# Four orders in the QKV stage: when rows are loaded and normalised, where two transposes stand, and when keys are split

## The reference

```python
x = x + _L0_xattn_ref(_layernorm(x, axis=-1), ...)
...
def rat_read(res, W, gamma, beta, num_outputs):
    x = res.reshape(b, l, H, C)                      # H = 512, C = 4
    y = jnp.einsum('blhc,hoc->bloh', x, W)
    mu = y.mean(-1, keepdims=True)
    var = y.var(-1, keepdims=True)
    yn = (y - mu) * jax.lax.rsqrt(var + EPS)
    yn = yn * gamma.reshape(num_outputs, H) + beta.reshape(num_outputs, H)
...
qkv_in = rat_read(hidden_states, attn_read_w, attn_read_g, attn_read_b, 3)
q, k, v = jnp.split(qkv_in, 3, axis=-1)
q = jnp.einsum('bli,oi->blo', q, qkv_w[0]).reshape(b, l, NH, HD)   # and k, v alike; NH = 16, HD = 32
q = rope(q, pos)
k = rope(k, pos)
```

## Time and profile before

| | us |
|---|---|
| median of 3 runs | 2207.84 |
| lowest and highest run | 2196.89, 2216.57 |
| the profiled execution | 2209.95 |
| its span, first to last instruction | 2208.0 |
| PE busy | 2082.5 (94%) |
| DVE busy | 1489.1 (67%) |
| ACT busy | 1085.5 (49%) |
| POOL busy | 1165.4 (53%) |

### The profile page before, as it was taken

How to read it: one execution, slowest core, us unless ns; L and a number is a source line. 1 busy time by engine, 2 the same in 40 slices (tenths; PEclk the granted TensorE clock), 3 DMA queues, 4 the chain that set the end, 5 groups by cost and what they waited for, 6 DMA issues and landing times.

```text
span 2208.0 us, 32471 instructions
## 1 busy us (share of the span) xinstructions
PE 2082.5 (94%) x11176; PEld 1702.9 (77%) x11176; DVE 1489.1 (67%) x1982; ACT 1085.5 (49%) x1700; POOL 1165.4 (53%) x717
## 2 busy tenths in 40 slices
PE   6988889999997999799999999999889999999999
PEld 4777766666665888688888899999678878888877
DVE  6787766777775999445655526776876675757663
ACT  3444447888895888621322336666633232323221
POOL 0111127899897888400000068776666676666564
PEclk9999997999998999899999999999999999999999
DMA  5678763333323766377998648778988699897895
GB/s 191 210 236 254 234 211 97 103 102 103 106 75 114 284 246 236 144 252 247 312 324 267 231 175 303 295 286 308 335 327 294 227 314 333 279 308 251 269 310 198
DMA packets 259994, 518.21 MB, mean 235 GB/s; under 512 B 21081, under 2 KB 136793, under 8 KB 241282
## 3 DMA queue, kind: packets, MB, share of 16 engines
q1 hardware_dynamic: 259842, 516.24, 69.9%
HBM read 360.45 MB, written 155.45 MB: 234 GB/s over the span
## 4 chain that ended last, share of the span: by engine, by line
PE 74%; DVE 8%; DMA 5%; ACT 5%; issue 4%; POOL 3%; SPq 1%; DVEq 0%; POOLq 0%; ACTq 0%
PE s_m_psG L2359 8%; PE s_m_psU L2359 8%; PE s_psF L2955 7%; PE s_psF L2957 7%; PE s_psF L2956 7%; PE s_psO L923 6%; PE s_w_psA L1923 4%; PE s_w_psB L1923 4%; PE s_psS L868 4%; PE s_psX L898 3%; DMA s_f_xs<-xnT 2%; PE s_psQ L575 2%; PE s_psQ L577 2%; PE s_psQ L576 2%; PE s_psY L559 2%
## 5 line engine op out<-in xcount | busy, mean ns | idle before, releaser
L1068 POOL TENSOR_TENSOR s_a_pl<-s_a_pf,s_a_ph 128x1024 fp32r<-128x1024 f32 (+1 forms) x128 | 279.8, 2214 | 35.0 <-ACT s_a_pf L1024 34.9
L2911 POOL TENSOR_TENSOR s_f_xs<-s_f_xl,s_f_xs 128x1024 f32<-128x1024 f32 x80 | 204.1, 2551 | 147.5 <-DMA s_f_xs<-xnT 147.2
L2095 POOL TENSOR_TENSOR s_w_yl<-s_w_y,s_w_yh 128x1024 fp32r<-128x1024 f32 x32 | 76.1, 2404 | 366.1 <-ACT s_w_yh L2003 366.1
L951 DVE TENSOR_REDUCE s_a_mx<-s_psS 128x1 f32<-128x896 f32 (+2 forms) x248 | 179.3, 754 | 77.7 <-PE s_psS L874 77.6
L2784 ACT ACTIVATE s_f_xh<-s_f_xs 128x1024 fp32r<-128x1024 f32 x80 | 84.9, 1061 | 291.0 <-POOL s_f_xs L2911 289.1
L2835 DVE TENSOR_TENSOR s_f_xl<-s_f_xs,s_f_xh 128x1024 fp32r<-128x1024 f32 x80 | 110.0, 1375 | 163.4 <-ACT s_f_xh L2784 163.4
L2955 PE MATMUL s_psF<-s_f_wh,s_f_xh 128*128 128x512 f32 x448 | 175.7, 392 | 8.1 <-DVE s_f_acc L2852 7.5
L448 POOL TENSOR_TENSOR s_q_qk<-s_q_ra,s_q_rb 128x1024 f32<-128x1024 f32 x16 | 37.8, 2361 | 275.2 <-DVE s_q_rb L691 275.2
L2957 PE MATMUL s_psF<-s_f_wh,s_f_xl 128*128 128x512 f32 x448 | 174.9, 390 | 0.0
L2956 PE MATMUL s_psF<-s_f_wl,s_f_xh 128*128 128x512 f32 x448 | 174.9, 390 | 0.0
L1021 ACT ACTIVATE s_a_ph<-s_psX 128x1024 fp32r<-128x1024 f32 (+1 forms) x160 | 150.2, 939 | 43.8 <-PE s_psX L903 40.0
(11 more groups left out here) (332 smaller groups left out, 6340.0 us busy)
## 6 DMA issues: line engine op xcount, KB each, us to landing
s_f_xl<-xnT SPq DMA_DIRECT2D x112, 512.0 KB, 5.3
s_f_xs<-xnT SPq DMA_DIRECT2D x80, 512.0 KB, 6.9
s_q_xt<-xT SPq DMA_DIRECT2D x16, 1024.0 KB, 7.4
s_q_xc<-xP SPq DMA_DIRECT2D x16, 1024.0 KB, 10.0
hsD<-s_q_hs SPq DMA_DIRECT2D x16, 1024.0 KB, 4.8
s_w_hin<-hsD SPq DMA_DIRECT2D x16, 1024.0 KB, 4.9
hs<-s_w_res SPq DMA_DIRECT2D x16, 1024.0 KB, 4.7
s_m_raw<-giT SPq DMA_DIRECT2D x32, 512.0 KB, 5.4
```

The source lines that it names most:

```text
L951: dve.tensor_reduce(mx[:, slot % 2, qi:qi + 1], psS[:, off:off + (qi + 1) * P], AX, ALU.max).then_inc(mx_ok, 1)
L1068: pool.tensor_tensor(pl[:, r, cols], pf[:, j - 1, 0:n], ph[:, r, cols], ALU.subtract).then_inc(pl_ok, 1)
L2911: pool.tensor_tensor(xs[i % 3][:], xl[u % 4][:].bitcast(F32), xs[i % 3][:], ALU.add if product(u)[1][1][2] > 0 else ALU.subtract).then_inc ...
```

## The change

Four orders of work change; no instruction is added or removed. SP loads xc of a tile as the first thing of a step, as soon as `hs_ok` of tile s-2 frees the buffer, and no longer behind the store of hs and the load of xt; each load now has a semaphore of its own. ACT runs `first_norm` in front of the split of the third output, and both parts of q and k are split in front of the outputs' square root. PE has the first two transposes between read 0 and read 1. DVE splits q and k in front of the rotation.

```diff
@@ sync
             def body(s, p, live):
+                if live(0):
+                    if (s - 2).exists():
+                        sp.wait_ge(hs_ok, count(s - 2, 1, 1))
+                    sp.sem_inc(k["settled"], 1)
+                    sp.dma_start(xc[:, p], io["xP"][ds(s.at(P), P), :]).then_inc(xc_in[p], 16)
                 if live(2):
                     sp.wait_ge(hs_ok, count(s - 2, 1, 1))
...
                         sp.wait_ge(y_mm, count(s - 2, 4, 4))
                     sp.sem_inc(k["settled"], 1)
-                    tok = s.at(P)
-                    sp.dma_start(xt[:, p], io["xT"][:, :, ds(tok, P)]).then_inc(x_in[p], 16)
-                    sp.dma_start(xc[:, p], io["xP"][ds(tok, P), :]).then_inc(x_in[p], 16)
+                    sp.dma_start(xt[:, p], io["xT"][:, :, ds(s.at(P), P)]).then_inc(xt_in[p], 16)
+                if live(0):
                     if at_slot(s, 0):
                         sp.dma_start(wraw[:], io["wqkv"]).then_inc(w_in, 16)
@@ scalar
                     hi_y(s, 1)
+                if live(1):
+                    first_norm(s, 1 - p)
                 if live(2):
                     hi_y(s, 2)
-                if live(1):
-                    first_norm(s, 1 - p)
                 if live(3):
                     hi_qk(s, 0)
+                    hi_qk(s, 1)
                 if live(1):
                     act.wait_ge(y_norm, count(s - 1, 11, Y_SQ))
...
-                if live(3):
-                    hi_qk(s, 1)
                 if live(2):
                     act.wait_ge(qkv_mm, count(s - 2, 3, 3))
@@ tensor
-                    pe.wait_ge(x_in[1 - p], dma_count(s - 1, 2, 2))
+                    pe.wait_ge(xt_in[1 - p], dma_count(s - 1, 2, 1))
...
                 if live(1):
                     read(s, p, 0)
-                    read(s, p, 1)
                 if live(2):
                     turn_y(s, 0)
                     turn_y(s, 1)
+                if live(1):
+                    read(s, p, 1)
+                if live(2):
                     project(s, 0)
@@ vector
-                dve.wait_ge(x_in[p], dma_count(s, 2, 2))
+                dve.wait_ge(xc_in[p], dma_count(s, 2, 1))
...
                        .then_inc(sh_ok, 1)
+                if live(3):
+                    lo_qk(s, 0)
+                    lo_qk(s, 1)
                 if live(2):
...
-                if live(3):
-                    lo_qk(s, 0)
-                    lo_qk(s, 1)
```

More of the change, by code:

```diff
@@ L389, in build_qkv @@
         Y_LESS, Y_AGG, Y_VAR, Y_INV, Y_SQ = 2, 8, 9, 10, 11
-        x_in = [sem(f"x_in{p}") for p in range(2)]
+        xt_in = [sem(f"xt_in{p}") for p in range(2)]
+        xc_in = [sem(f"xc_in{p}") for p in range(2)]
         y_mm = sem("y_mm")
```

## The result

| | before | with the change |
|---|---|---|
| median, us | 2210.06 (4 runs) | 2179.95 (4 runs) |
| lowest and highest run | 2196.89, 2216.57 | 2172.20, 2183.38 |
| the profiled execution | 2209.95 | 2178.96 |
| its span | 2208.0 | 2177.2 |
| steps 3 to 16, 14 of them | 242.06 | 210.43 |

The ratio of the medians is 0.9864, with a 95% interval of 0.9823 to 0.9904: 1.4% faster. The span became 30.8 us shorter.

A forecast was written before the change was run, and what follows sets the result against it. No engine filled the QKV steps (PE 88% busy); PE and DVE waited, largely for late xc. Terms -29.3 - 1.8 - 1.4 + 1.7 = -30.8 from 2209.95 gave 2179.1 us; it named 2178, range 2166 to 2200.

The forecast's parts named there:

- case A: Whole kernel: the forecast itself comes true, own range 2168 to 2188 us, chance 0.56.
- The step: QKV steps 3 to 16: 17.29 us falls to 15.03 at full clock, 15.2 taken; 14 steps give -29.3 us.
- Late normalisation as the cause of late xc: QKV step: xc's load waits for ACT's normalisation, done at T+12.9; moved, it runs T+3.0 to T+5.1, 7.8 us sooner.
- DVE's slack: QKV step: DVE's chain ends at T+17.05, its next split stands at T+17.18, slack 0.13 us, the tightest place.
- Rival B: QKV steps: DVE's chain becomes the bound, the keys' split wait returns every second step, step 15.97, 2190 us; chance 0.19.
- The rule on DMA order: SP's DMA queue: descriptors of a ring go in order, so hsD behind xc lands 4.8 to 10.0 us after issue.
- C: QKV steps: DMA engines become the bound, DVE waits again, steps about 16.5, 2197 us; chance 0.07.
- E: QKV steps: the hs buffer's loop closes late behind a 12.97 us xc issue, step 20.4, 2254 us; chance 0.04.
- Start: First steps: the second xc goes ahead of xt, the chain behind starts sooner, -1.4 us, bounds 0 and -2.0.
- Step 17: Outside the stretch, with step 2: each gets the reads' or psB gain, 0.88 us, together -1.8, bounds 0 and -3.
- Handoff: End of QKV: last rotations stand behind the key split, PE's wait for POOL grows 1.51 to 3.2, +1.7 us.
- rival D: Handoff to attention: longer wait lengthens PE's half-clock stretch by 20 us, +10 us allowed, 2188 us; chance 0.10.

The follow-up runs named there:

- the rows edit: Kernel before, plus only xc loaded first and the normalisation ahead of the third output's split: 2192.77 us, ratio 0.9925.
- the runs without reads: Changed kernel with read 1 back ahead of the two transposes, 2193.29 us; kernel before with only xc's load and the normalisation moved, 2192.77 us.
- the normalisation late: Changed kernel with only ACT's normalisation back behind the third output's split, xc still loaded first: 2183.95 us, ratio 0.9876.
- DVE's chain longer: Changed kernel plus two unused 128x256 DVE additions between the keys' split and the rotations, in steps that also load a tile: 2184.03 us.
- rows and normalisation undone: Changed kernel with xc loaded last again and the normalisation behind the third output's split: 2205.36 us, ratio 0.9976.
- reads undone: Changed kernel with read 1 back ahead of the two transposes: 2193.29 us, ratio 0.9925.
- the store of hs last: Changed kernel with the store of hs moved behind the load of xt: 2179.3 us (1 run).
- the change again: The changed kernel unaltered, run again beside the handoff kernels: 2178.40 us, ratio 0.9854.
- the products that kept PE at work: Changed kernel plus 24 unused products of the identity with itself on PE ahead of the last key transposes: 2178.09 us, ratio 0.9868.

## Why the prediction was right

It named 2178 us, with 2166 to 2200 around it, and 2179.95 was measured; by the medians the gain is 30.1 us, where 2207.84 - 2178 = 29.8 was forecast. The likeliest case A is what happened, for the reasons given. By its steps:

**The step.** Forecast T+2.94, T+6.01, T+6.45, T+8.56, T+11.96 and T+15.03 at full clock; the trace has T+2.92, 5.99, 6.42, 8.54, 11.94 and 15.02. The 0.30 that it left lost ahead of the first projection is 0.32 by the starts (185.58 - 184.39 less a read of 0.87), 0.15 of it a wait. I then took 15.2 for a granted clock of 0.99 and was 0.17 too long: the stretch came out at 1.00. The 0.99 of the earlier trace rows was the one low spot of the profiled execution of before, 3.4 us long, and nothing that a shorter step inherits. The same spot made the 17.29 too long by 1.6 / 14 = 0.11. Over 14 steps it is the largest miss on this side: -29.3 forecast, -31.6 measured, and about -30.0 without that spot.

**What causes which part.** The forecast put 30.3 us of DVE waits and with them PE's last-projection waits on the rows edit, and it does carry the bulk: 17.29 to 15.90 by itself, while the other two without it reach only 16.97. The reads' 0.88 of saving is 15.90 to 15.03 (with the split). That the split frees psB was right; that it should be needed only with the reads' move was not said, and the runs without reads show it.

**Late normalisation as the cause of late xc.** Half right. The normalisation's place does free the buffer 7.7 us sooner (it starts at T+3.03, forecast T+3.0). But with it undone and the load first xc is still in time. What the early place then buys is quiet in SP's queue ahead of the stores of q and k, which the forecast did not have.

**DVE's slack.** 0.13 forecast, 0.13 read between the two rows above, 0.23 by the run with two additions. Rival B, a step of 15.97, did not come: the steps of the change differ among themselves by 0.02 us.

**The rule on DMA order.** The forecast had hsD land between 4.8 and 10.0 us after its issue. It landed after a median of 8.6, and 3.8 when it was issued first again. The Trainium skill (DMA: Bandwidth & Descriptors, Queues, rings and completion order) has each DMA engine take the descriptors of a ring in order, and the traces agree. The later landing costs nothing, as forecast: 2.6 + 0.37 + 0.35 + 8.6 = 11.9 us is under 15.03, and the normalisation never waits for it, so rivals C and E fall. E's long issue of 12.97 does have a kin in the steady stretch, 7.86, but only with the normalisation late, and then on the stores of q and k.

**Start.** -1.4 for the first steps and -0.9 for step 2, -2.3 in all, against -2.58 measured from PE's first instruction to step 3.

**Step 17.** -0.9 forecast, -0.36 measured. There is no read in this step, so the reads' move gives nothing there, and PE waited 1.66 us for DVE ahead of the projection. I had counted the reads' or the psB gain outside the stretch without looking which of them that step has. This term was mis-sized.

**Handoff.** +1.7 forecast and +3.1 measured, outside its bounds of 1.3 and 2. This is the term that was furthest off for its size. The order's part was right: the wait for POOL is 3.15 (forecast 3.2), 1.64 more. The term left out the clock: 1.4 us over attention's first products, which had run at full clock behind the shorter wait. Where the clock stayed up behind the longer wait too, in the run with DVE's chain longer, the term is 43.57 - 42.07 = +1.5. The forecast had this as rival D at +10; the mechanism was there and its price a seventh of that. The low stretch grew from 27.3 us (327.1 to 354.4) to 34.1 (289.9 to 324.0), where D had 20 more, and from the load of the keys on both kernels run alike.

The sum by these terms is -29.3 - 2.3 - 0.9 + 1.7 = -30.8, and the spans differ by 30.8. Part of that agreement is luck: the steps gave 2.3 more and the start 0.3, the handoff and step 17 1.9 less, and of what no term had, the landing of the first loads took 1.4 and the rest of the program gave 0.7. The 1.6 of the low spot in before is in the 2.3, so that most of what the steps gave more is luck too.

## What to carry to other kernels

Follow one step of a pipeline engine by engine with the durations of its own trace, and close each loop; with PE's order written out, the step at full clock came right to 0.01 us, and what was mis-sized lay outside the loop, in the clock and in the last step. Price an early load by what its issue then stands next to, too: the same edit moved three megabytes away from small stores that another engine waits for. And look at the place where the pipeline ends by itself: an order that is best in the loop can be the wrong one in its last turn, where nothing covers it.

## What the hardware showed that I had not expected

The issue of a quarter of a megabyte on SP took up to 7.86 us in the steady stretch when three megabytes were issued within 1.3 us ahead of it, and at most 1.4, mostly 0.4, with the change, where they start over 3.2 us. In the kernel before, the third of three issued within 1.5 us took 2.4 to 3.8 itself. DVE operations that follow each other directly overlap by 0.07 to 0.08 us, so that a chain is shorter than the sum of its durations.

Eight of the traces here have the wait of 3.15 us at the handoff: the two of the change, rows and normalisation undone, the two with one of these undone, reads undone, the store of hs last and DVE's chain longer. In seven the granted clock fell to half between 0.4 us before that wait ended and 1.2 us behind it. In the eighth, DVE's chain longer, it fell only 5.5 us behind it, so the long wait does not settle it alone. Where the wait was 1.51 to 1.55, 0.17 or none, the clock held for 4.9 to 8.1 us more in all six traces. It then stayed low for 24 to 38 us, although PE was busy for 4.88 of 5.00 us in one such stretch; in two traces (the change again, and the normalisation late) a first fall was over after some 3.5 us and the clock fell again 3.4 to 6.8 us later. What ends it these runs do not show, and whether the low stretch could be avoided altogether was not settled: the products that kept PE at work only put it off.
